# Moved POOL work, a reordered router chain and a new order of two lanes in a two-layer perceiver kernel

## The chip, the core and the metric

The kernel runs on one core of one Trainium2 chip, in one launch. Five engines take part: TensorE (PE), VectorE (DVE), ScalarE (ACT), GpSimd (POOL) and SyncE (SP). Each has its own instruction queue, works through it in order, and waits on semaphores that the others raise. The metric is the device time of one execution in microseconds.

## The reference, cut to what matters

Four sequences of 128 latents with 128 channels (`x`) pass through two layers; a context of 2048 tokens per sequence is attended to in each. Each step adds its result to `x`, after a normalisation of its input.

```python
# layer 0: sampled cross attention (A), retention (B), expert layer (C)
gate_scores = softmax(x @ Wg.T)                    # 8 experts
topk_val, topk_idx = top_k(gate_scores, 2)
comb = one_hot(topk_idx) weighted by topk_val / (topk_val.sum() + EPS)
for e in range(8):
    a, b = split(x @ W1[e].T + b1[e]); g = a * sigmoid(b)
    out = out + (g @ Wo.T + bo) * comb[..., e:e + 1]
# layer 1: masked cross attention (D), a gated retention block (E), expert layer (F)
scores = where(mask == 0, -1e9, q @ k.T / sqrt(8)); out = softmax(scores) @ v
# E: convolution over the batch, silu, q k v g, 2-way router per head, rotary,
#    causal retention, a norm per head, gate, projection, then a silu feed-forward block
# F: router over 8 experts (top 2), gelu(x @ w1[e]) @ w2[e] weighted and summed
```

## The kernel before

**Stages.** `STAGES` A to E follow each other; E holds the second retention and the last expert layer too. The 512 tokens stand as four blocks `b` of 128. Everything is float32 apart from some helpers in bf16. PSUM is one tensor `BK` of 8 banks. The order on each engine is written out by hand as a list of calls, and each call waits on counted semaphores.

**Stage B** is the first retention. PE computes scores (L2058), DVE multiplies them by the decay (L1370), PE multiplies by the values (L2067). `b_s_ps` counts the scores. POOL is nearly idle here.

**Stage C**, the first expert layer. After the norm PE computes the router's logits (L2099). DVE turns them into weights in some twenty small instructions (L1402 to L1432), ACT does one Exp (L797), and `r_cw` counts two marks of DVE: the sum of the weights, and the weights split into three bf16 parts in `CW3`. PE transposes these (L2125), ACT copies them (`CWS`, L801, `c_split`), and `widen_share(e)` (L2117) spreads the weights of expert e over the partitions. Meanwhile `up(e)` (L2109) makes the four hidden tiles of an expert, two pairs (a, b); ACT takes the sigmoid of the b tile (L807), `gated(e, j)` on DVE multiplies (L1397, counted by `e_g`), and `share(e, j)` multiplies by the spread weights (L1440, counted by `c_part`). POOL adds the results of experts 1 to 5 into `SUM` (L631, `c_sum`). PE projects `SUM`, expert 6 and expert 7 with `joined` (L2136) into four banks. Its `proj_ps` marks let DVE add the residual, two blocks at a time (L1024, `both_added`), and begin the next norm.

POOL has other work in stage C: `keys_and_values` builds the block-diagonal keys `QB` (L603), the values `VMD` and `ONEH` for stage D, and L623 and L625 prepare the bias and residual in `XH` that the last add uses.

**Stage D**, the masked cross attention over the last 128 keys, in 16 steps n of four heads. ACT takes the exponentials (L821), PE transposes (`turn(n)`, L2196), ACT or DVE copies the result back (`turned(n)`, L830 or L1737), and `values(b)` (L2212) multiplies by the values (c = 0) and by ones (c = 1, the softmax sums). `divide(b)` (L1475) divides. `project_keys(h)` (L2223, L2227) projects and `looked_up(h)` (L1731) adds.

**Stage E** runs in two lanes h of two blocks each, interleaved with stage D and with each other. Lane h goes through `first_stats`, norm LN_E (L1536), transposes (`lane_norm_T`, L2271), `convolve`, `gate_xT`/`gated_xT`, `project_qkvg` (L2278), `choices`, `shares`, `rotate` on POOL, `weights`, `outputs`, `centred`, `square`, `variances`, `deviation` (a Sqrt), `contexts`, `turn_context`, `project_context`, `attended`, norm LN_E2, `ff_up` (L2302), `gate_ff` (a Tanh) and `gated_ff`, `ff_down` (L2311), `finished`, norm LN_F, `logits`, `chances`, `route` (an Exp), `best_two`. Then come its eight experts: `up(h, e)` (L2329), `gelu(h, e)` (L906), `down(h, e)` (L2344), `weigh(h, e)` (L1724). `down(h, e)` waits for `weigh(h, e - 2)`, since two experts share a bank. Lane 1 is one retention behind lane 0: its retention runs beside the experts of lane 0.

**Warming.** `stay_warm(bk, n)` (L1829) issues n matmuls of the identity whose result nobody reads. `WARM` is 13. ACT holds one set of function tables at a time; a function outside it gets an ACT_TABLE_LOAD ahead of it.

## Time and profile before

| | us |
|---|---|
| runs of the kernel | 279.26, 281.15, 281.96 (median 281.15) |
| the profiled execution | 281.34 |
| its span, first to last instruction | 279.6 |
| busy in the span: PE, DVE, ACT, POOL | 235.5, 191.2, 128.1, 43.2 |
| mean granted TensorE clock | 0.933 |

The profile records one execution. An engine's busy time is the time of its instructions; register, branch, semaphore and DMA-issuing instructions are not counted. A float32 matmul stands as two instructions in the trace. The granted clock is 1.0 at 2.4 GHz and 0.5 at 1.2 GHz.

### The profile page before, as it was taken

Reading aid. Unit: us, or ns where it says so; the run is one execution under the profiler, and the core shown is the slowest. Engines: PE = TensorE matmul, PEld = TensorE weight load, DVE = VectorE, ACT = ScalarE, POOL = GpSimd, SP = SyncE. Lnnn points to the kernel's source line nnn. Section 1 sums busy time; section 2 is a strip of 40 time slices with the busy share of each in tenths; the row PEclk is TensorE's granted clock in tenths of the full one; section 3 lists DMA queues with packets and bytes.
Section 4 is the critical chain, followed back from the end, with each engine's and each line's share of the span. In section 5 each row is a group of like instructions: output and inputs, shape, how many; then the busy total and the mean of one; then the engine's idle time right before and its main releaser. Section 6 shows DMA issues by size and latency. Waiting matters only on the chain.

```text
span 279.6 us, 4964 instructions
## 1 busy us (share of the span) xinstructions
PE 235.5 (84%) x1885; PEld 171.5 (61%) x1885; DVE 191.2 (68%) x550; ACT 128.1 (46%) x274; POOL 43.2 (15%) x65
## 2 busy tenths in 40 slices
PE   8858676957869679699995998759878999999995
PEld 8445453635434565244592564437666999999995
DVE  6998899587578667979866768785779655424111
ACT  1377785644161106233305955762424564363331
POOL 6000000000100038367320001210350010100000
PEclk9999998695597999999999999986995999999999
DMA  6970000003980300000000000000000000000000
GB/s 179 356 295 1 2 4 0 2 2 83 438 382 1 147 6 0 2 0 0 0 4 1 2 2 1 1 2 0 4 0 0 0 4 0 2 0 19 2 0 19
DMA packets 5564, 13.74 MB, mean 49 GB/s; under 512 B 2081, under 2 KB 3745, under 8 KB 4898
## 3 DMA queue, kind: packets, MB, share of 16 engines
q1 hardware_dynamic: 4096, 10.73, 10.3%
q10 hardware_dynamic: 1442, 2.66, 2.9%
q8 instruction: 16, 0.26, 0.4%
q14 instruction: 10, 0.08, 0.1%
HBM read 13.13 MB, written 0.26 MB: 48 GB/s over the span
## 4 chain that ended last, share of the span: by engine, by line
PE 60%; DVE 23%; ACT 9%; issue 4%; POOL 1%; DMA 1%; DVEq 0%; ACTq 0%
PE BK L2329 11%; PE BK L2344 10%; PE BK L2109 7%; PE BK L2212 3%; PE BK L2185 3%; ACT WTF L750 3%; PE BK L2196 2%; DVE WTF L1370 2%; PE BK L1932 2%; PE BK L2136 2%; DVE WTF L1215 2%; PE BK L1829 2%; PE BK L2058 2%; ACT WTF L821 1%; PE BK L2041 1%
## 5 line engine op out<-in xcount | busy, mean ns | idle before, releaser
L2329 PE MATMUL BK<-XT,WTF 128*128 128x256 f32 x128 | 32.8, 404 | 0.0
L2344 PEld LDWEIGHTS BK<-WTF 128*128 128x128 f32 x256 | 30.9, 192 | 0.8
L906 ACT ACTIVATE WTF<-BK 128x512 f32<-128x512 f32 x32 | 18.9, 598 | 26.4 <-PE BK L2329 26.4
L2344 PE MATMUL BK<-WTF 128*128 128x128 f32 x256 | 31.0, 275 | 0.0
L2109 PE MATMUL BK<-XT,WTF 128*128 128x512 f32 x64 | 28.7, 594 | 0.0
L2329 PEld LDWEIGHTS BK<-XT,WTF 128*128 128x128 f32 x128 | 25.0, 205 | 3.2
L1724 DVE SCALAR_TENSOR_TENSOR X<-BK,CW,X 128x128 f32<-128x128 f32 x32 | 9.7, 346 | 24.7 <-PE BK L2344 24.7
L750 ACT ACTIVATE WTF<-BK 128x512 f32<-128x512 f32 x40 | 22.6, 601 | 7.1 <-PE BK L1915 7.0
L597 POOL TENSOR_TENSOR RSTD<-VE,MHALF 128x2 f32<-128x2 f32 x8 | 5.6, 710 | 103.9 <-DVE VE L1043 103.1
L821 ACT ACTIVATE WTF<-BK,MN 128x128 f32<-128x128 f32 x64 | 18.0, 394 | 6.7 <-DVE MN L1469 6.7
L2109 PEld LDWEIGHTS BK<-XT,WTF 128*128 128x128 f32 x64 | 12.0, 190 | 14.1 <-issue 12.8
L1215 DVE TENSOR_SCALAR WTF<-WTF 128x512 f32<-128x512 f32 x40 | 16.5, 421 | 4.9 <-ACT WTF L750 4.5
L807 ACT ACTIVATE KVW<-BK,cols_sb 128x512 f32<-128x512 f32 x16 | 11.0, 688 | 17.7 <-PE BK L2109 17.7
L1932 PE MATMUL BK<-WTF,KVW 128*32 128x160 f32 x256 | 12.9, 326 | 5.8 <-DVE WTF L1215 5.6
L1915 PE MATMUL BK<-R,SELR 128*128 128x128 bf16 x160 | 14.1, 230 | 4.1 <-DVE R L1120 4.1
L1915 PEld LDWEIGHTS BK<-R,SELR 128*128 128x128 bf16 x160 | 10.4, 103 | 9.1 <-issue 5.9
L2196 PE MATMUL BK<-ident,WTF 128*128 128x128 f32 x64 | 10.4, 292 | 5.3 <-ACT WTF L830 2.6
L638 POOL TENSOR_TENSOR RSTD<-VE,MHALF 128x2 f32<-128x2 f32 x6 | 4.2, 700 | 69.0 <-DVE VE L1530 43.6
L2196 PEld LDWEIGHTS BK<-ident,WTF 128*128 128x128 f32 x64 | 7.1, 145 | 11.6 <-ACT WTF L821 8.8
L1397 DVE SCALAR_TENSOR_TENSOR WTF<-BK,cols_sb,KVW 128x512 f32<-128x512 f32 x16 | 11.9, 747 | 3.1 <-ACT KVW L807 3.1
L631 POOL TENSOR_TENSOR WTF<-WTF 128x512 f32<-128x512 f32 x10 | 12.5, 1274 | 8.7 <-DVE WTF L1440 8.7
L1465 DVE TENSOR_REDUCE MX<-BK 128x4 f32<-128x512 f32 x16 | 11.0, 686 | 4.1 <-PE BK L2185 4.1
(309 smaller groups left out, 457.7 us busy)
## 6 DMA issues: line engine op xcount, KB each, us to landing
WTF<-w_f_dram SPq DMA_DIRECT2D x2, 2048.0 KB, 14.5
WTF<-w_c_dram SPq DMA_DIRECT2D x1, 2048.0 KB, 7.7
decay<-c_decay_dram ACTq DMA_DIRECT2D x1, 1024.0 KB, 7.3
decay<-mask_q_dram SPq DMA_DIRECT2D x1, 1024.0 KB, 4.8
crows_sb<-c_rows_dram ACTq DMA_DIRECT2D x1, 544.0 KB, 8.1
w_e_sb<-w_e_dram SPq DMA_DIRECT2D x1, 480.0 KB, 4.8
w_b_sb<-w_b_dram SPq DMA_DIRECT2D x1, 384.0 KB, 5.5
WTF<-win_dram SPq DMA_DIRECT2D x1, 320.0 KB, 6.2
```

The source lines that it names most:

```text
L631: pool.tensor_tensor(SUM[:, j, :], SUM[:, j, :], GT[:, e % 2, 2 + j, :], ALU.add).then_inc(c_sum, 1)
L750: act.activation(WT[:, v % 2, :, :, k, :], sbank(u).rearrange("p (h u q) -> p h u q", h=4, u=4), ACT.Abs)\
L821: ins = act.activation(SS[:, b % 2, h, :], score_bank(n)[:, j * P:(j + 1) * P], ACT.Exp, scale=float(1.0 / np.sqrt(HD)), bias=MN[:, b, h:h ...
L906: act.activation(GT[:, e % 2, 2 * p:2 * p + 2, lane_cols(h)], lane_bank(h, 2 + p).rearrange("p (a n) -> p a n", a=2), ACT.Gelu).then_inc(e ...
L1215: dve.tensor_scalar(w, w, 1.0, -1.0, ALU.min, ALU.add).then_inc(a_w, 1)
L1397: dve.scalar_tensor_tensor(out=GT[:, e % 2, j, :], in0=hbank(2 * p), scalar=ba, in1=SG[:, e % 2, j, :], op0=ALU.add, op1=ALU.mult).then_in ...
L1915: ins = pe.matmul(sbank(u)[:, h * P:(h + 1) * P], SEL[:, NK * h + k, :], R[:, g, a * P:(a + 1) * P], start=True, stop=True)
L1932: ins = pe.matmul(BK[32 * h:32 * h + 32, sample_bank(n), j * NK * QL:(j + 1) * NK * QL], KVW[:, 2 * b + j, 4 * g + h, :, :].rearrange("p f ...
L2109: ins = pe.matmul(hbank(u), w_c1[:, o:o + P], XT[:, :], start=True, stop=True)
L2196: ins = pe.transpose(turn_bank(n)[:, h * P:(h + 1) * P], SS[:, b % 2, 4 * g + h, :], ident[:, :])
L2329: ins = pe.matmul(lane_bank(h, 2 + p)[:, 256 * i:256 * i + 256], w_f1[:, o:o + P], XT[:, lane_cols(h)], start=True, stop=True)
L2344: ins = pe.matmul(lane_bank(h, e % 2)[:, i * P:(i + 1) * P], GT[:, e % 2, j, b * P:(b + 1) * P], w, start=(j == 0), stop=(j == 3))
```

## The change

On POOL the keys and values for stage D are built in stage B, as soon as the buffers are free; the values come first, so the counts of `d_blk` change. L623 and L625 move behind the adds of the experts. The power of LN_F of lane 0 is done in the middle of `rotate(1)`. In stage C half of `up(2)` stands ahead of the wait for `c_split`, the last `widen_share` stands between the halves of `up(7)`, DVE does `share(7, 0)` before `gated(7, 1)`, and the last `joined` is split by `j`. In stage D and E two tiny activations load the tables of Sqrt and Gelu early, `values(3)` is split by `c` around the projection of context 0, the order of the lanes on ACT, DVE and PE changes, and `route(1)` moves behind `gelu(1, 1)`. Warming matmuls: 13 become 11 ahead of stage C, 10 ahead of stage D and 10 ahead of LN_F; the 8 after `project_keys(1)` go.

```diff
-            def keys_and_values():
-                pool.wait_ge(b_o_ps, 4)
+            def last_values():
+                pool.wait_ge(a_ctx, 4)
+                settle(pool.memset(VMD, 0.0))
+                settle(pool.memset(ONEH[:, :, :], 0.0))
+                pool.memset(own(ONEH[:, :, :]), 1.0).then_inc(d_blk, 1)
+                pool.wait_ge(vd_ready, 1)
+                pool.tensor_copy(own(VMD), vd[:, :, :].rearrange("p b (g j d) -> p (b g) j d", g=4, j=4))\
+                    .then_inc(d_blk, 1)
+
+            def last_keys():
+                pool.wait_ge(b_s_ps, 16)
                 pool.wait_ge(kd_ready, 1)
...
                 if s == "B":
                     power(LN_B)
                     pool.memset(CW3[:, :, :, :], 0.0).then_inc(consts_ready, 1)
+                    last_values()
+                    last_keys()
                 if s == "C":
                     power(LN_C)
-                    pool.wait_ge(ln_xhat, xhat_count(LN_C))
-                    keys_and_values()
...
+                    pool.wait_ge(r_cw, 1)
+                    pool.wait_ge(ln_xT_ps, xT_count(LN_C))
+                    pool.wait_ge(loads["crows"], 48)
+                    settle(pool.tensor_tensor(XH[:, :, :], row("ff_bo").unsqueeze(1).to_broadcast([P, B, D]),
+                                              S1[:, :].unsqueeze(2).to_broadcast([P, B, D]), ALU.mult))
+                    pool.tensor_tensor(XH[:, :, :], XH[:, :, :], X[:, :, :], ALU.add).then_inc(xb_ready, 1)
...
                         settle(pool.tensor_tensor(qr, qk, cs[:, 0, pair], ALU.mult))
+                        if meanwhile:
+                            lane_power(*meanwhile)
...
-                    rotate(1)
-                    lane_power(LN_F, 0)
+                    rotate(1, (LN_F, 0))
...
                     exponentials(15)
+                    act.activation(VM[:, :], col("eps"), ACT.Sqrt)
                     turned(14)
                     turned(15)
                     square(0)
                     deviation(0)
+                    act.activation(VM[:, :], col("eps"), ACT.Gelu)
                     context(0)
                     second_xT(0)
+                    gate_ff(0, (0,))
                     gate_xT(1)
-                    gate_ff(0)
+                    gate_ff(0, (1, 2))
                     take_qkvg(1)
+                    last_xT(0)
+                    gelu(0, 0)
                     between(1)
-                    last_xT(0)
+                    gelu(0, 1)
                     route(0)
-                    gelu(0, 0)
-                    gelu(0, 1)
                     square(1)
                     gelu(0, 2)
                     deviation(1)
                     gelu(0, 3)
+                    gelu(0, 4)
                     context(1)
...
                     for e in range(NE):
                         gelu(1, e)
+                        if e == 1:
+                            route(1)
...
+                        if e == NE - 1:
+                            share(e, 0)
+                        if e >= 2:
                             gated(e, 1)
-                        share(e, 0)
+                        if e < NE - 1:
+                            share(e, 0)
...
                     contexts(0)
+                    attended(0)
                     divide(3)
-                    attended(0)
+                    lane_norm(LN_E2, 0, CT)
                     looked_up(1)
                     first_stats(1)
-                    lane_norm(LN_E2, 0, CT)
                     lane_norm(LN_E, 1, X)
                     convolve(1)
+                    gated_ff(0, (0,))
                     gated_xT(1)
-                    gated_ff(0)
+                    gated_ff(0, (1, 2))
                     gated_q(1)
                     finished(0)
+                    lane_norm(LN_F, 0, X)
                     choices(1)
+                    chances(0)
                     shares(1)
-                    lane_norm(LN_F, 0, X)
                     gate_out(1)
                     weights(1)
-                    chances(0)
                     outputs(1)
+                    centred(1)
                     best_two(0)
-                    centred(1)
                     bypass(1)
                     variances(1)
                     weigh(0, 0)
+                    weigh(0, 1)
                     contexts(1)
...
+                    up(2, (0, 1))
                     pe.wait_ge(c_split, 1)
                     widen_share(0)
-                    for e in range(1, NE):
+                    widen_share(1)
+                    up(2, (2, 3))
+                    for e in range(2, NE - 1):
                         widen_share(e)
-                        if e + 1 < NE:
-                            up(e + 1)
+                        up(e + 1, (0, 1) if e == NE - 2 else range(4))
+                    widen_share(NE - 1)
+                    up(NE - 1, (2, 3))
...
+                    pe.wait_ge(c_part, 2 * NE - 1)
+                    for b in range(B):
+                        joined(last, b, False, False, (0,))
                     pe.wait_ge(c_part, 2 * NE)
                     for b in range(B):
-                        ins = joined(last, b, False, True)
+                        ins = joined(last, b, False, True, (1,))
...
-                    values(3)
+                    values(3, (0,))
                     turn_context(0)
                     project_context(0)
+                    values(3, (1,))
                     project_keys(1)
-                    stay_warm(3, 8)
                     lane_norm_T(LN_E2, 0, 1)
                     lane_norm_T(LN_E, 1, 1)
                     ff_up(0)
                     project_qkvg(1)
                     ff_down(0)
-                    stay_warm(3)
+                    stay_warm(3, 10)
                     lane_norm_T(LN_F, 0, 0)
```

Beside the experts of lane 0, each step of lane 1 (`turn_context(1)`, `project_context(1)`, its norms, `ff_up(1)`, `ff_down(1)`) stands one expert later on PE, and `down(0, 7)` comes ahead of `logits(1)` and `up(1, 0)`; ACT and DVE follow the same order.

## Rows read from the trace of the kernel before

**Rows 1.** Page, part 2: granted clock in 40 slices of the span.

```profile
PEclk9999998695597999999999999986995999999999
```

**Rows 2.** Chain that ended last, in order of time: start, us, what.

```profile
138.80 5.36 PE BK L2136 x48
...
212.18 6.08 PE BK L2329 x16
...
220.04 1.73 PE BK L2329 x8
```

**Rows 3.** Timeline of the router chain: start, us, engine, line, operation, count, idle before.

```profile
101.90 1.37 POOL L597 TENSOR_TENSOR RSTD<-VE,MHALF 128x2 f32<-128x2 f32 x2 [29.37 <-DVE VE L1043]
...
103.98 4.03 POOL L603 TENSOR_TENSOR SCR<-kTd,head_sb 128x512 f32<-128x512 f32 x4 [0.72 <-DVE XH L999]
...
107.29 0.77 DVE L1407 TENSOR_TENSOR PR<-EX,S 128x32 f32<-128x32 f32 x1
...
112.01 0.18 DVE L1423 CAST SELR<-RK 128x32 bf16<-128x32 f32 x1
...
112.36 1.04 POOL L623 TENSOR_TENSOR XH<-rows_sb,S 128x512 f32<-128x512 f32 x1 [1.61 <-DVE S L1424]
112.45 0.98 DVE L1427 CAST SELR<-EX 128x32 bf16<-128x32 f32 x1
...
113.48 1.26 POOL L625 TENSOR_TENSOR XH<-XH,X 128x512 f32<-128x512 f32 x1
114.02 0.78 DVE L1431 CAST R<-SELR 128x64 f32<-128x64 bf16 x1
...
114.95 0.64 PE L2125 MATMUL BK<-ident,R 128*96 128x128 f32 x4 [1.89 <-DVE R L1432]
...
116.28 0.60 PE L2117 MATMUL BK<-SELR,gate 96*128 96x512 bf16 x2 [0.69 <-ACT SELR L801]
```

**Rows 4.** Timeline at the end of stage C.

```profile
140.01 1.28 DVE L1440 TENSOR_TENSOR WTF<-BK,WTF 128x512 f32<-128x512 f32 x2
143.38 0.43 DVE L1024 TENSOR_TENSOR X<-BK,XH 128x256 f32<-128x256 f32 x1 [2.09 <-PE BK L2136]
```

**Rows 5.** Timeline from the last turn of stage D to `ff_down(0)`.

```profile
187.90 0.60 ACT L830 ACTIVATE WTF<-BK 128x512 f32<-128x512 f32 x1 [1.27 <-PE BK L2196]
...
188.81 1.28 ACT L874 ACT_TABLE_LOAD   x1
...
190.11 0.32 ACT L874 ACTIVATE SM<-SM,cols_sb 128x32 f32<-128x32 f32 x1
190.26 1.93 PE L2212 MATMUL BK<-WTF,ONEH 128*32 128x128 f32 x32
...
192.25 0.96 DVE L1475 RECIPROCAL KEEP<-BK 128x128 f32<-128x128 f32 x1 [0.91 <-PE BK L2212]
...
195.74 0.42 DVE L1731 TENSOR_TENSOR X<-BK,X 128x256 f32<-128x256 f32 x1 [0.28 <-PE BK L2227]
...
203.46 1.60 PE L2311 MATMUL BK<-w_e_sb,decay 128*128 128x128 f32 x12 [0.30 <-DVE decay L1679]
```

**Rows 6.** Timeline from `shares(1)` to `down(0, 2)`.

```profile
208.88 0.19 DVE L1594 SCALAR_TENSOR_TENSOR SM<-SCR 128x32 f32<-128x32 f32 x1
...
209.48 0.60 DVE L1536 TENSOR_SCALAR XH<-X,MV,RSTD 128x128 f32<-128x128 f32 x2
...
210.14 0.55 PE L2271 MATMUL BK<-ident,XH 128*128 128x128 f32 x2 [2.17 <-DVE XH L1536]
...
220.65 0.61 DVE L1724 SCALAR_TENSOR_TENSOR X<-BK,CW,X 128x128 f32<-128x128 f32 x2
...
225.34 1.95 PE L2344 MATMUL BK<-WTF 128*128 128x128 f32 x16
```

**Rows 7.** Windows: us, then busy of PE, PEld, DVE, ACT, POOL; clock, DMA, GB/s.

```profile
151.50:153.64 2.14, 0.00 (x1) 0.00 (x1) 2.06 (x5) 1.34 (x6) 0.00 (x0) 1.00 0.00 0
...
210.35:217.20 6.85, 6.38 (x18) 5.06 (x17) 6.17 (x19) 3.08 (x5) 0.00 (x0) 0.50 0.00 0
```

More of the change, by code:

```diff
@@ L616, in _ @@
                     pool.memset(CW3[:, :, :, :], 0.0).then_inc(consts_ready, 1)
+                    last_values()
+                    last_keys()
                 if s == "C":
                     power(LN_C)
-                    pool.wait_ge(ln_xhat, xhat_count(LN_C))
-                    keys_and_values()
-                    pool.wait_ge(r_cw, 1)
-                    pool.wait_ge(loads["crows"], 48)
-                    settle(pool.tensor_tensor(XH[:, :, :], row("ff_bo").unsqueeze(1).to_broadcast([P, B, D]),
-                                              S1[:, :].unsqueeze(2).to_broadcast([P, B, D]), ALU.mult))
-                    pool.tensor_tensor(XH[:, :, :], XH[:, :, :], X[:, :, :], ALU.add).then_inc(xb_ready, 1)
                     for e in range(1, NE - 2):
@@ L644, in _, with rotate @@
                     flat = lambda a: a.rearrange("p b a n -> p b (a n)")
-                    def rotate(h):
+                    def rotate(h, meanwhile=None):
                         pair = lane_pair(h)
@@ L950, in _ @@
                     gelu(0, 3)
+                    gelu(0, 4)
                     context(1)
-                    gelu(0, 4)
+                    gelu(0, 5)
                     second_xT(1)
-                    gelu(0, 5)
+                    gelu(0, 6)
                     gate_ff(1)
-                    gelu(0, 6)
+                    gelu(0, 7)
                     last_xT(1)
-                    gelu(0, 7)
-                    route(1)
                     for e in range(NE):
                         gelu(1, e)
+                        if e == 1:
+                            route(1)
         @block.vector
@@ L2126, in _, with joined @@
                     ins.then_inc(c_wide_ps, 1)
+                    up(2, (0, 1))
                     pe.wait_ge(c_split, 1)
                     widen_share(0)
-                    for e in range(1, NE):
+                    widen_share(1)
+                    up(2, (2, 3))
+                    for e in range(2, NE - 1):
                         widen_share(e)
-                        if e + 1 < NE:
-                            up(e + 1)
-                    def joined(src, b, start, stop):
-                        for j in range(2):
+                        up(e + 1, (0, 1) if e == NE - 2 else range(4))
+                    widen_share(NE - 1)
+                    up(NE - 1, (2, 3))
+                    def joined(src, b, start, stop, js=(0, 1)):
+                        for j in js:
                             ins = pe.matmul(BK[:, (2, 3, 4, 6)[b], 0:P], src(j)[:, b * P:(b + 1) * P],
@@ L2197, in turn, with values @@
                         ins.then_inc(d_pT_ps, 1)
-                    def values(b):
+                    def values(b, cs=(0, 1)):
                         pe.wait_ge(d_pT, (2, 4, 8, 12)[b])
@@ L2203, in values @@
                         if b == 0:
-                            pe.wait_ge(d_blk, B + 2)
+                            pe.wait_ge(d_blk, 2)
                         if b == 3:
                             pe.wait_ge(d_om, 3)
-                        for c in range(2):
+                        for c in cs:
                             for j in range(4):
```

42 lines of the change are left out of this document (18 added, 24 removed).

## The prediction

> **What bounds the kernel now.** I read the clock row of the page first: TensorE is granted full speed nearly everywhere, with dips around slices 10, 13, 27 and 31 [rows 1]. Then the chain that ended last, in order of time. It runs on PE through the first expert layer, where the eight experts end in one unbroken piece of 48 matmul instructions, 5.36 us, and again from 212.18 to the end of the span, where each further expert step of 8 instructions takes 1.73 us [rows 2]. The first 16 instructions of that last stretch took 6.08 us; at 1.73 us for 8 they would take 3.46. So there are two kinds of place where time can be won: the stretches in which PE waits before such a piece begins, and the low-clock stretches. The timeline then shows who is late in each place, and windows show the clock [rows 3 to 7].
>
> **Part 1, the router chain.** Between the logits and the weights that `widen_share` spreads, DVE works through a string of tiny instructions. A cast of 32 columns takes 0.18 us; three of the tiny ones took 0.77, 0.98 and 0.78 us instead, and each ended within 0.1 us of the end of a POOL `tensor_tensor`: L1407 at 108.06 beside L603 (to 108.01), L1427 at 113.43 beside L623 (to 113.40), L1431 at 114.80 beside L625 (to 114.74) [rows 3]. That is (0.77-0.18) + (0.98-0.18) + (0.78-0.18) = 2.0 us of waiting for POOL. The change takes all three POOL jobs away: L603 and its neighbours go to stage B, L623 and L625 go behind the adds of the experts. So `r_cw` comes at 112.9, not 114.9.
>
> The second gain is PE's hole. The four transposes end at 115.59 and the first `widen_share` starts at 116.28, after ACT's copy [rows 3]: 0.69 us. `up(2, (0, 1))` now stands in it; what it needs (`e_g` 2) is `gated(0, 1)`, which DVE does before `r_cw`. I count 0.6 of it. Sum of part 1: -2.6 us for PE at the start of the experts. Does it last? PE is busy without a break from there to 144.16, and DVE finishes the last share at 141.29 (L1440, 140.01 + 1.28), 1.0 us before PE reaches the matmuls that need it, at about 142.3 [rows 2, 4]. DVE's shares start only about 0.9 us earlier than now, since `widen_share(0)` comes behind half of `up(2)`, so DVE loses 1.7 us of its distance in the first experts. The 1.0 us at the end is the way of the last pair itself (PE, sigmoid, `gated`, `share`), not a backlog of DVE, so I expect it to stay; if the 1.7 were carried to the end, PE would wait 0.7 and -1.9 would be left. I keep -2.6; the bounds are -0.6 (POOL was not the cause) and -2.7.
>
> **What the moved POOL work costs in stage B.** POOL is idle for 29.37 us before the power of LN_C at 101.90 [rows 3]. `last_values` (memset 1.8 us, a copy) falls where DVE has nothing pressing. `last_keys` waits for the last scores, about 91.2, and its 4.03 us end at 95.3, ahead of the power that is queued behind it. Beside it DVE runs operations that read PSUM; L1440, of the same kind, takes its 0.64 us in the expert stage, where POOL adds all the time [rows 4]. Cost 0; if one were held, at most one POOL instruction, 1.0 us. The keys' other waiters are in stage D, long after. If `last_keys` came 7 us late it would hold the power of LN_C.
>
> **Part 2, the last pair.** `share(7, 0)` before `gated(7, 1)` and the split of `joined(last, ...)` shorten the way from the last share to the projection. But PE gets there last, 1.0 us after DVE (above), so nothing waits that could be shortened: 0. The split has a price instead. Now the two matmuls of block 0 and of block 1 precede those of 2 and 3, so the first half is free four matmuls before the end; DVE starts its add at 143.38, 0.8 us before PE ends [rows 4]. With `js` outermost it is free only two before the end. 48 instructions in 5.36 us [rows 2] are 0.22 us for each of the 24 matmuls, so this is +0.45 us for the add, and all that follows to the norm of stage D hangs on it. The 10 warming matmuls in place of 13 then just make sure that PE is not late itself: 0. Bounds for part 2: 0 to +0.45; I take +0.45, since nothing but DVE's and POOL's own short steps stands between that add and the norm.
>
> **Part 3, the end of the second retention.** Times are those of the profile of before. (a) A dummy Sqrt now stands ahead of `turned(14)`. The table load is 1.28 us and the tiny activation about 0.2 us, so `turned(14)`, `turn(15)`, `turned(15)` (187.90) and `values(3)` come 1.5 us later [rows 5]. In exchange `deviation(0)` finds its table there: the load at 188.81 goes. Context 0 is ready at about 192.1, and `project_context(0)` keeps its place. (b) The second half of `values(3)`, 1.93 us at the low clock and about half at the full one, now follows it, so `divide(3)` starts at 195.5 to 196.0 where it started at 192.25, and `looked_up(1)` moves from 195.74 to 197.6 to 198.1: +1.9 to +2.4 us [rows 5]. On PE `ff_up(0)` is queued behind the transposes of that lane's norm, so `ff_up(0)` and `ff_down(0)` (203.46) move by the same amount; I take +1.9. (c) The norm of LN_F of lane 0 now follows its statistics at once, on DVE and on POOL (in the middle of `rotate(1)`, whose rest waits meanwhile, with `weights(1)` behind it, which is not due until later). PE's wait of 2.17 us ahead of the transposes at 210.14 nearly goes: -2.1 [rows 6]. (d) Then the experts may start at 211.4 instead of 212.18, at full clock: -0.8 and -2.6. But DVE is late next. `between(1)` stands behind `gelu(0, 0)`, so `shares(1)` can start at about 211.4 + 1.73 + 1.0 = 214.1. From its first instruction at 208.88 to the end of the first `weigh` (220.65 + 0.61) DVE took 12.4 us, of which some 1.2 are the norm, the chances and pauses [rows 6]. So `weigh(0, 0)` ends at 214.1 + 11.2 = 225.3, and `down(0, 2)`, which needs it, started at 225.34 before [rows 6]. The 3.4 us are waited away there. From there both orders are PE work without a break, and the later order of lane 1 and of `route(1)` (two table loads beside PE's 3.5 us per expert) adds no wait. Part 3: 0, with bounds -0.8 and +0.5 while the clock behaves.
>
> What a table load costs decides (a). The trace has the load at 188.81 and the next activation at 190.11, 1.30 us later [rows 5]. The Trainium skill ("ScalarE: Activation LUTs", What ACT_TABLE_LOAD costs) adds a drain of about 1.38 us to every switch, 2.66 us in all; by that, `values(3)` would come 2.9 us later and the sum would be 1.4 us worse. The row shows no such drain.
>
> **Sum.** The profiled execution took 281.34 us, span 279.6 and 1.74 around it, which stays. 281.34 - 2.6 + 0.45 + 0 = 279.2 us. It lies 0.2 above the median of the three runs, 281.15; I keep 279.2.
>
> **The rivals.**
> *Clock, slower side.* The change drops 8 warming matmuls between `project_keys(1)` and the next transposes, and leaves PE idle there for about 2.4 us (198.2 to 200.6 by the moves above); after the start of the second experts it leaves another pause of 2.6 us while `gelu(0, 2)` and `weigh(0, 0)` are late. PE's pause of 2.17 us before 210.14 was followed by the low level, 1.2 GHz, in the window from 210.35 to 217.20; a pause of 2.14 us at 151.50 was not [rows 7]. So it can go either way. One such stretch over work that bounds costs 6.08 - 3.46 = 2.6 us [rows 2]: 279.2 + 2.6 = 281.8. It decides when PE rests over some 2 us in one of the two places with the clock falling behind it; both together give 284.4. The Trainium skill ("TensorE: Matmul & The Clock Gate", Part 1) says that half rate is the default and that activity releases it; by that rule alone removed warming matmuls can only hurt, with the same 281.8.
> *Lane order wins.* If the Sqrt and the second half of `values(3)` hide better than I think, so that `looked_up(1)` is not later, the 2.1 us of (c) are kept: 279.2 - 2.1 = 277.1. For it: in (b) the low clock makes up nearly 1 us. Against it: three engines' queues all put lane 1 behind `values(3)`.
> *It doesn't do what it says.* The three long DVE instructions are long for another reason than POOL. Then part 1 is -0.6 and the time is 281.34 - 0.6 + 0.45 = 281.2. Against it: three coincidences within 0.1 us.
>
> **Chances.** Forecast 0.42 (278.4 to 280.2 by its bounds), clock 0.27, lane order 0.23, not POOL 0.08. The range reaches into the rivals on both sides, to 277.0 and to 282.8. About 1% (2.8 us) is what a measurement of this kernel can tell from no change. Faster by more means below 278.3: nearly all of the lane-order case and a little of the forecast, 0.27. Slower means above 284.0: both clock stretches, 0.10. Within: 0.63.
>
> **What would show it.** In the profile of the changed kernel: L1407, L1427 and L1431 at about 0.2 us, and no gap between the transposes and `up(2)`; the experts of the first layer starting 2.6 us earlier and still that much ahead at their end; the first add of stage D less than 0.5 us before PE's end; a table load ahead of `turned(14)`; `looked_up(1)` late and PE idle before the transposes of lane 1; no 2.17 us pause before LN_F; a wait of PE for ACT and DVE before `up(0, 3)` and `down(0, 2)`. The prediction is wrong if the clock falls in one of those pauses, or if DVE's distance in the first experts is used up, so that PE waits for `gated` there.

## The result and the profile after

The changed kernel takes 289.38 us, the median of four executions (287.37 to 290.95). The kernel before, timed beside it, took 281.55 us. The ratio is 1.0306 with a 95% interval of 1.024 to 1.0373: slower by 3%. Here and in the table of the experiments a median is that of all executions, while a ratio leaves out those over 1.5% above the fastest of their kernel. The profiled execution of the changed kernel took 287.37 us, with a span of 285.6 us.

The clock row of its page answers to [rows 1].

```profile
PEclk9999997997799799999996899955599989999999
```

Slices 27 to 29, 7.1 us each, stand at half speed, where before had an 8, a 6 and a 9; slice 22 has a 6, where before had a 9. The low slices of before at 8, 10, 11 and 31 are higher here. The slices count from 1. The granted clock averaged over the four executions is 0.911. I cut both traces at the same events to see where the 6.0 us between the two profiles arose. The times in this table are starts of instructions, the last one the end of the last operation ahead of the output DMA; the last column is the run e5, explained with the experiments.

| stretch, from one event to the next | before | after | difference | values late |
|---|---|---|---|---|
| start to the norm of stage B | 71.28 | 69.55 | -1.7 | 69.53 |
| to the norm of stage C | 31.34 | 33.42 | +2.1 | 30.13 |
| to the norm of stage D | 43.48 | 41.06 | -2.4 | 41.07 |
| to the second part of `values(2)` | 35.21 | 38.35 | +3.1 | 38.39 |
| to `up(0, 0)` | 30.72 | 33.60 | +2.9 | 30.12 |
| to `down(0, 2)` | 13.31 | 15.18 | +1.9 | 12.17 |
| to the end | 52.02 | 52.23 | +0.2 | 52.02 |

**Router chain.** The timeline of the changed kernel answers to [rows 3], this time with the router instructions alone:

```profile
107.63 0.19 DVE L1416 TENSOR_TENSOR PR<-EX,S 128x32 f32<-128x32 f32 x1
112.20 0.18 DVE L1436 CAST SELR<-EX 128x32 bf16<-128x32 f32 x1
112.96 0.18 DVE L1440 CAST R<-SELR 128x64 f32<-128x64 bf16 x1
113.30 0.64 PE L2139 MATMUL BK<-ident,R 128*96 128x128 f32 x4
141.31 0.42 DVE L1033 TENSOR_TENSOR X<-BK,XH 128x256 f32<-128x256 f32 x1 [2.73 <-PE BK L2154]
```

All three long instructions are short, and stage C is 2.4 us shorter. The last row is the first add of stage D: PE ended at 141.65, so it starts 0.34 us before PE's end where in the kernel before it started 0.78 us ahead [rows 4].

**Stage B.** The timeline around its norm:

```profile
70.47 2.22 DVE L1008 TENSOR_SCALAR XH<-X,MV,RSTD 128x128 f32<-128x128 f32 x2 [0.33 <-POOL RSTD L597]
70.74 1.81 POOL L601 MEMSET KEEP<- 128x2048 f32 x1
72.69 0.44 PE L1836 MATMUL BK<-ident,XH 128*128 128x128 f32 x2 [2.15 <-DVE XH L1008]
73.87 5.40 PE L2055 MATMUL BK<-XT,w_b_sb 128*128 128x512 f32 x8 [0.75 <-ACT XT L702]
```

The second pair of the norm takes 2.22 us, and it ends 0.14 us after the end of the moved memset of `VMD` on POOL. PE waits 2.15 us for it. Behind that pause the clock is low, as the windows below show. In the kernel before, the same memset stood in stage C, beside instructions of the router chain, and held none of those that began behind it. L1409 took 0.43 us beside it, and the same instruction takes 0.43 us in the changed kernel with no memset beside it:

```profile
107.95 1.80 POOL L605 MEMSET KEEP<- 128x2048 f32 x1
108.10 0.43 DVE L1409 TENSOR_TENSOR SELR<-PR 128x256 f32<-128x256 f32 x1
```

**End of the retention.** The chain that ended last, in order of time, from the dummy Sqrt (L938) to `ff_down(0)` (L2333):

```profile
187.23 1.28 ACT L938
188.72 0.49 ACT WTF L835
189.35 1.10 PE BK L2217 x4
...
194.32 1.22 PE BK L2314 x4
195.54 1.87 PE BK L2233 x32
197.41 1.15 PE BK L1847 x2
198.55 1.15 PE BK L2245 x4
199.71 0.87 PE BK L2249 x4
201.05 0.50 DVE STAT L1534 x2
...
203.56 0.69 PE BK L2293 x2
204.25 4.11 PE BK L2324 x12
```

Windows of it: us, then busy of PE, PEld, DVE, ACT, POOL; clock, DMA, GB/s.

```profile
74.00:77.40 3.40, 3.40 (x5) 1.32 (x6) 0.69 (x1) 0.00 (x0) 0.09 (x1) 0.51 1.00 429
152.80:159.20 6.40, 6.40 (x20) 3.16 (x19) 3.00 (x6) 3.84 (x15) 0.00 (x0) 0.50 0.00 0
186.80:207.20 20.40, 14.27 (x98) 10.32 (x97) 10.98 (x36) 6.72 (x14) 2.73 (x4) 0.50 0.00 1
227.70:231.10 3.40, 3.40 (x8) 2.77 (x9) 3.16 (x12) 3.28 (x4) 0.00 (x0) 0.50 0.00 0
```

For 20.4 us without a break TensorE has 1.2 GHz. In this stretch the links that run on PE cost 1.5 to 1.8 times what they do at 2.4 GHz: the projections 1.22 us instead of 0.71, a half of `values` 1.94 instead of 1.06. `looked_up(1)` comes at 200.60 (before: 195.74 [rows 5]), `ff_down(0)` at 209.73 (203.46). What `divide(3)` waits for is the second half of `values(3)`, as its row in the timeline says:

```profile
195.47 1.94 PE L2233 MATMUL BK<-WTF,ONEH 128*32 128x128 f32 x32
195.58 0.42 DVE L1680 TENSOR_TENSOR CT<-BK,WTF 128x256 f32<-128x256 f32 x1 [2.48 <-PE BK L2314]
197.47 0.96 DVE L1488 RECIPROCAL KEEP<-BK 128x128 f32<-128x128 f32 x1 [0.47 <-PE BK L2233]
```

**Experts of lane 0.** Timeline of the changed kernel, against [rows 6]:

```profile
214.60 0.44 PE L2293 MATMUL BK<-ident,XH 128*128 128x128 f32 x2 [1.03 <-DVE XH L1549]
...
225.28 0.42 ACT L875 ACTIVATE WTF<-WTF 128x256 f32<-128x256 f32 x1 [3.35 <-DVE WTF L1651]
225.71 1.28 ACT L911 ACT_TABLE_LOAD   x1
...
227.66 2.93 PE L2351 MATMUL BK<-XT,WTF 128*128 128x256 f32 x6 [2.59 <-ACT WTF L911]
```

`up(0, 3)` waits 2.59 us for `gelu(0, 2)`, which stands on ACT behind `square(1)`; that one waits 3.35 us for DVE's chain of lane 1.

### The profile page after: what moved, and what is told of

It is laid out like the page before. It is cut to its first block, busy times and chain, and to the rows that moved or that the text cites. A ratio compares the mean times of both kernels' runs of the same rounds, so it can differ in the third digit from the quotient of the medians.

```text
span 285.6 us, 4904 instructions
## 1 busy us (share of the span) xinstructions
PE 235.7 (83%) x1853; PEld 168.9 (59%) x1853; DVE 190.9 (67%) x550; ACT 129.4 (45%) x277; POOL 43.3 (15%) x65
## 4 chain that ended last, share of the span: by engine, by line
PE 58%; DVE 23%; ACT 11%; issue 3%; POOL 2%; DMA 1%; DVEq 0%; ACTq 0%; POOLq 0%
PE BK L2123 10%; PE BK L2351 9%; PE BK L2366 9%; PE BK L2206 3%; DVE WTF L1379 3%; ACT WTF L755 3%; PE BK L2233 3%; PE BK L2217 3%; PE BK L2324 2%; PE BK L2154 2%; POOL RSTD L597 2%; PE BK L1946 2%; DVE WTF L1224 2%; ACT WTF L826 1%; PE BK L2197 1%
## 5 line engine op out<-in xcount | busy, mean ns | idle before, releaser
L2351 PE MATMUL BK<-XT,WTF 128*128 128x256 f32 x128 | 32.1, 398 | 2.6 <-ACT WTF L911 2.6
L2351 PEld LDWEIGHTS BK<-XT,WTF 128*128 128x128 f32 x128 | 24.0, 199 | 6.3 <-ACT WTF L911 3.2
L2123 PEld LDWEIGHTS BK<-XT,WTF 128*128 128x128 f32 x64 | 12.0, 190 | 13.3 <-issue 12.2
L1224 DVE TENSOR_SCALAR WTF<-WTF 128x512 f32<-128x512 f32 x40 | 16.5, 420 | 4.6 <-ACT WTF L755 4.2
L2217 PE MATMUL BK<-ident,WTF 128*128 128x128 f32 x64 | 11.8, 321 | 6.7 <-ACT WTF L835 4.0
L1929 PE MATMUL BK<-R,SELR 128*128 128x128 bf16 x160 | 13.4, 222 | 4.1 <-DVE R L1129 4.1
L2217 PEld LDWEIGHTS BK<-ident,WTF 128*128 128x128 f32 x64 | 8.1, 160 | 13.8 <-ACT WTF L826 7.0
L1929 PEld LDWEIGHTS BK<-R,SELR 128*128 128x128 bf16 x160 | 9.7, 98 | 9.0 <-issue 5.8
L702 ACT ACTIVATE XT<-BK 128x512 f32<-128x512 f32 x4 | 2.4, 597 | 24.2 <-PE BK L1836 21.9
## 6 DMA issues: line engine op xcount, KB each, us to landing
WTF<-w_f_dram SPq DMA_DIRECT2D x2, 2048.0 KB, 14.4
```

Source lines behind the costliest of these rows:

```text
L1224: dve.tensor_scalar(w, w, 1.0, -1.0, ALU.min, ALU.add).then_inc(a_w, 1)
L1929: ins = pe.matmul(sbank(u)[:, h * P:(h + 1) * P], SEL[:, NK * h + k, :], R[:, g, a * P:(a + 1) * P], start=True, stop=True)
L2123: ins = pe.matmul(hbank(u), w_c1[:, o:o + P], XT[:, :], start=True, stop=True)
L2217: ins = pe.transpose(turn_bank(n)[:, h * P:(h + 1) * P], SS[:, b % 2, 4 * g + h, :], ident[:, :])
L2351: ins = pe.matmul(lane_bank(h, 2 + p)[:, 256 * i:256 * i + 256], w_f1[:, o:o + P], XT[:, lane_cols(h)], start=True, stop=True)
```

## The experiments

The result of each is the median, and the ratio to the kernel before on the same chip with its 95% interval. "Clock" is the granted clock averaged over the executions; that of before was 0.937 to 0.941 in these runs, two executions of 352 and 568 us left out.

| run | median us | ratio | interval | clock |
|---|---|---|---|---|
| e1 router | 284.78 | 1.0195 | 1.0066 to 1.0323 | 0.921 |
| e2 lanes | 286.98 | 1.0224 | 1.0102 to 1.0347 | 0.918 |
| e3 warm | 286.23 | 1.0216 | 1.0069 to 1.0363 | 0.931 |
| e4 no dummy | 288.72 | 1.0262 | 1.0103 to 1.0422 | 0.914 |
| e5 values late | 279.62 | 0.9965 | 0.9927 to 1.0002 | 0.943 |
| e6 late, warm | 279.87 | 0.9956 | 0.9910 to 1.0002 | 0.940 |
| e7 whole join | 280.10 | 0.9980 | 0.9935 to 1.0025 | 0.933 |
| e8 POOL only | 284.27 | 1.0135 | 1.0067 to 1.0204 | 0.929 |
| e9 retention half | 284.95 | 1.0124 | 1.0044 to 1.0204 | 0.916 |
| e10 expert half | 280.17 | 0.9957 | 0.9910 to 1.0003 | 0.940 |
| e11 norm early | 281.92 | 1.0014 | 0.9972 to 1.0056 | 0.938 |
| e12 no eight | 282.14 | 1.0038 | 0.9989 to 1.0087 | 0.927 |
| e13 no dummies in e9 | 284.41 | 1.0134 | 1.0090 to 1.0179 | 0.920 |
| e14 whole values in e9 | 284.00 | 1.0095 | 1.0057 to 1.0133 | 0.928 |
| e16 expert half mended | 279.42 | 0.9941 | 0.9909 to 0.9972 | 0.941 |
| e17 order only | 283.48 | 1.0107 | 1.0063 to 1.0151 | 0.926 |
| e18 changed, values late | 285.22 | 1.0155 | 1.0086 to 1.0223 | 0.919 |

### The two halves, the warming and the dummies

The theory at this point: the memset on POOL takes back most of the router's gain, and the order at the end of the retention is late by itself. The rivals: the missing warming matmuls are the whole cause, or one half of the change is.

e1 has parts 1 and 2 (POOL's moves in stages B and C, the router order, the last pair, warming of 11 and 10), with the lanes of before.

> Parts 1 and 2 alone: the POOL moves, the router chain, the last pair, 11 and 10 warming matmuls; stage D and E in the order of before. Theory A (hold and order): the memset in stage B takes back 1.6 us, the chain gives 2.5 us, the split of the join takes 0.45, and the low stretch at the start of stage D (3.1 us) is a result of the shorter warming and the new timing there: 281.5 + 1.6 - 2.5 + 0.45 = 281.1 us without that stretch, 284 with it. Rival 1 (the lane order is all of it): 279.5. Rival 2 (warming is the cause everywhere): 284.

e2 has part 3 only, with stages A to C of before.

> Part 3 alone: the order of the lanes, the two dummy activations, values(3) split, the 8 warming matmuls gone; stages A to C as before. Theory A: values(3) comes 1.6 us later, looked_up(1) 4.9 us later, and both lanes start the last experts late: 281.5 + 6 = 287.5 us. Rival 1 (all of it is here): 289.5. Rival 3 (nothing of it is here, it's clock luck in stages B to D): 281.5.

e3 is the changed kernel with all its warming back.

```diff
-stay_warm(3, 11)
+stay_warm(3)
-stay_warm(1, 10)
+stay_warm(1)
 project_keys(1)
+stay_warm(3, 8)
-stay_warm(3, 10)
+stay_warm(3)
```

> The changed kernel with the warming matmuls of before: 13, 13, 8 after project_keys(1), 13. Rival 2 (the clock falls because PE rests where warming was taken away): 282 us, with the full clock from 190 us on. Theory A: the order is late by itself; the 8 matmuls shorten the low stretch after 187 us a little and cost nothing: 287 to 289 us.

e4 is the changed kernel without the two dummy activations.

```diff
-act.activation(VM[:, :], col("eps"), ACT.Sqrt)
-act.activation(VM[:, :], col("eps"), ACT.Gelu)
```

> The changed kernel without the two dummy activations, so turned(14) is not held by the table load. If the load ahead of turned(14) is the first cause of the delay (values(3) +1.6 us and the pause that lets the clock fall): 285 to 287 us, the full clock back before 200 us. If the split of values(3) and the order behind it are the cause: 289 us as the changed kernel, since deviation(0) then loads its table itself.

e1 and e2 are both slower than before, by 2.0% and 2.2%, so neither rival of a single half holds. The full warming gives back 0.9 points of the 3.06 (2.5 us), and e3 stays clearly slower than before, so missing warming isn't the whole cause; whether it is any part, e3 can't tell, since its interval reaches from 1.0069 to 1.0363. Without the dummies 0.4 points are gone, which the intervals can't tell from zero either.

### The memset in stage B

e5 is e1 with one semaphore changed: POOL's memset now waits until the rotary products of stage B are done.

```diff
 def last_values():
-    pool.wait_ge(a_ctx, 4)
+    pool.wait_ge(b_rot, 2)
     settle(pool.memset(VMD, 0.0))
```

> Parts 1 and 2, with the memset of the values on POOL held until the rotary products of stage B are done, so that it runs beside DVE operations that read PSUM. Nothing else differs from the router kernel. Theory (the memset holds the second pair of the norm of stage B for 1.6 us, and PE's pause behind it lowers the clock): the pair of TENSOR_SCALAR takes 0.6 us again, the stage starts 1.6 us earlier, 1.6 to 2.5 us less than the router kernel, which was 284.8 us: 282.3 to 283.2. Rival (the hold is absorbed later in stage B, where DMA or the scores set the pace): 284.5.

e5 takes 279.62 us, e1 284.78, a gain larger than either theory had. The timeline of e5, against the one of the changed kernel:

```profile
70.45 0.60 DVE L1003 TENSOR_SCALAR XH<-X,MV,RSTD 128x128 f32<-128x128 f32 x2 [0.33 <-POOL RSTD L597]
70.92 0.52 PE L1830 MATMUL BK<-ident,XH 128*128 128x128 f32 x2 [0.41 <-DVE XH L1003]
...
72.18 3.70 PE L2049 MATMUL BK<-XT,w_b_sb 128*128 128x512 f32 x8 [0.74 <-ACT XT L701]
...
77.73 1.80 POOL L601 MEMSET KEEP<- 128x2048 f32 x1 [6.95 <-DVE KEEP L1361]
78.96 1.29 DVE L1374 TENSOR_TENSOR WTF<-BK,decay 128x512 f32<-128x512 f32 x2 [1.28 <-PE BK L2066]
```

The pair takes 0.60 us again, and the projections behind it 3.70 us where the changed kernel needed 5.40, at the higher clock: the window from 74.0 to 77.4 stands at 1.00 here and at 0.51 there. Both profiles reach this norm at the same time, 69.53 and 69.55, so this is a clean comparison: the last column of the table has stage B 3.3 us shorter. The memset now runs mostly in a pause of DVE; the first of two products that read PSUM overlaps its last 0.6 us, and the two keep their 0.65 us each.

Between e1 and e5 the medians differ by 5.2 us and the ratios by 2.3 points, where e1's interval alone is 1.3 points wide to either side. Of this 1.6 us are the hold, and the average clock of the executions rose from 0.921 to 0.943. The profiles bear out more than the hold. From the norm of stage B to that of stage D all five with the memset at this norm (changed kernel, e1, e3, e4, e8) take 74.2 to 74.5 us; the twelve that have both the later memset and the router order take 70.3 to 72.5, 71.3 on average. So it costs about 3 us there, half of it the hold. That the pause is what lowers the clock is likely, not shown: all five have a low stretch that begins 1.2 to 1.6 us after PE's pause, but e2 and e14 have one at the same place (76.3 and 76.4) without the hold, and in both profiles of before and in e6 and e12 the clock is low there already.

e8 is before with POOL's moves alone, the early memset included.

> Before, with the POOL moves alone (values and keys in stage B, the two bias and residual jobs behind the adds); PE, DVE and ACT in the order of before, all warming as before. Theory: the three router instructions take 0.2 us each, weights 2.0 us earlier, but the memset holds the norm of stage B for 1.6 us: sum -0.4, 281.0 us. Rival (POOL was not the cause of the long router instructions): they stay at 0.8 us, 283 us.

It is 1.35% slower, 284.27 us where 281.0 was expected, with the router 2 us shorter (from the norm to the transposes 10.33 us, before 12.33) and the norm's pair again at 2.22 us. From the norm of stage B to that of stage D its profile has 74.45 us, before 74.82: hold and gain nearly cancel, as expected. What makes it slower than before stands ahead of the norm of B (1.2 us) and behind that of D (1.3 us), outside the steps that it moves.

e18 makes the same one-line repair in the changed kernel.

> The changed kernel (289.4 us) with one edit, the memset of the values waits for the rotary products of stage B. If the costs add up as in the router kernel (5.2 us there): 284.2 us. If there is only the hold itself of 1.6 us and the rest of the difference was chance: 287.8 us.

285.22 us instead of 289.38: 4.2 us, near the value that adds up.

### Warming and the join in stage C

e6 is e5 with 13 warming matmuls in place of 11 and 10.

> As the values-late kernel, with 13 warming matmuls ahead of stage C and of stage D instead of 11 and 10. Theory (the shorter warming lets the clock fall more often, at 153 and 98 us): mean clock over the executions back from 0.92 to 0.94, 280.0 us. Rival (the falls are chance): the same as the values-late kernel, 282.5 us.

279.87 against 279.62 us: no effect of that warming can be measured there. The theory that its lack made the clock fall is not borne out. e7 is e6 with the last join whole.

```diff
-pe.wait_ge(c_part, 2 * NE - 1)
-for b in range(B):
-    joined(last, b, False, False, (0,))
 pe.wait_ge(c_part, 2 * NE)
 for b in range(B):
-    ins = joined(last, b, False, True, (1,))
+    ins = joined(last, b, False, True)
```

> As the one before (late values, 13 and 13), with the join of the last pair whole again, all four matmuls of a block together. Forecast of the split's price: the first add of stage D starts 0.8 us before PE's end instead of 0.34, and the time is 0.45 us less: 279.5 us. Rival (the split lets PE start half of the join before the last share is done, and saves that wait): equal, or 0.3 us more.

280.10 against 279.87 us. The 0.45 us that the trace shows for the split is too small for this comparison, in either direction.

### Part 3 in halves, on a sound base

The base for what follows is e6, 279.87 us. e9 adds the end of the retention, with the 8 warming matmuls kept.

> Base is the kernel with late values and 13 and 13 warming matmuls (279.9 us), all 8 warming matmuls after project_keys(1) kept. Added: only the first half of part 3, the order at the end of the retention (two dummy activations, values(3) split around the projection of context 0, attended(0) and the norm LN_E2 ahead of divide(3) and looked_up(1), gate_ff split). Theory (this order is late by itself: from values(2) to the start of the last experts the changed kernel with full warming took 31.0 us where before took 30.7, though its early norm LN_F should save 2.1): +2.4, 282.3 us. Rival (only the missing warming made it late): 279.9 us.

e10 adds the early norm of LN_F and the new order of the experts.

> Same base (279.9 us). Added: only the second half of part 3, the norm LN_F of lane 0 right behind its statistics, between(1) behind gelu(0, 0), and lane 1 one expert later on PE, ACT and DVE. Theory (the early norm saves 2.1 us, but the first gelus stand ahead of between(1), shares(1) to centred(1) start late and with them square(1), gelu(0, 2) and weigh(0, 0): from the start of the experts to down(0, 2) 15.1 us where the base takes 12.2): -2.1 + 2.9 = +0.8, 280.7 us. Rival (PE is busy there anyway): 277.8 us.

e12 takes only the 8 warming matmuls out of the base.

> Same base (279.9 us), only the 8 warming matmuls after project_keys(1) taken away. Theory (the 3.1 us between the changed kernel and the one with full warming come from these 8): the clock stays low from about 190 to 205 us, mean clock 0.93 instead of 0.943, 282.5 us. Rival (the clock falls there because of the late order, the 8 don't matter): 279.9 us.

The first half costs 1.7 points (4.7 us), twice the expected 2.4 us. The second costs nothing. Taking the 8 matmuls out costs 0.8 points (2.3 us), near the 2.6 expected; the two intervals just overlap. In e12 PE pauses 2.10 us ahead of the transposes, where the base pauses 0.31 us, and the windows that follow stand at different levels, first e12's, then the base's:

```profile
200.00:203.60 3.60, 3.60 (x11) 2.68 (x10) 2.22 (x6) 1.82 (x4) 0.00 (x0) 0.54 0.02 5
```

```profile
200.00:203.60 3.60, 3.60 (x17) 2.59 (x15) 2.96 (x8) 2.44 (x5) 0.22 (x1) 1.00 0.01 2
```

`ff_up(0)` takes 4.44 us in e12 and 2.75 us in the base.

### Which piece of the retention half

e13 is e9 without the dummies, e14 is e9 with `values(3)` whole ahead of `turn_context(0)`, e17 is e9 with both undone. Only this is left in e17:

```diff
 contexts(0)
-divide(3)
 attended(0)
+divide(3)
+lane_norm(LN_E2, 0, CT)
 looked_up(1)
 first_stats(1)
-lane_norm(LN_E2, 0, CT)
 lane_norm(LN_E, 1, X)
```

with `gate_ff(0)` and `gated_ff(0)` split around the same step of lane 1.

> The retention half (285.0 us, ratio 1.0124) without its two dummy activations. Theory S (the table load ahead of turned(14) makes PE pause and lowers the clock over all that follows): turn(15) and values(3) 1.5 us earlier, full clock before 195 us, 281.5 us. Theory V (the second half of values(3) in front of project_keys(1) is what costs): the delay of lane 1 stays and deviation(0) loads its table itself, 284 to 285 us.

> The retention half (285.0 us) with values(3) whole ahead of turn_context(0), dummies kept. Theory V: divide(3) 2 us earlier and with it looked_up(1), 282 us. Theory S: the clock falls anyway, and context 0 now waits for all of values(3): 285 us or more.

> The retention half (285.0 us) without the dummies and with values(3) whole: what is left is attended(0) and the norm LN_E2 ahead of divide(3) and looked_up(1) on DVE, and gate_ff(0) split on ACT. Theory (the dummy Sqrt and the split of values(3) hold the loss between them, each brings its own late turn or late lane 1 and the low clock makes both dearer): the base again, 279.9 us. Rival (the order on DVE costs: divide(3) now waits for the projection of context 0, and project_keys(1) behind it comes 1 to 2 us later): 282 us.

Neither repair brought much. e13 came out where theory V had it, but e14, which takes V's cause away, came out at 284.00 us where V had 282. e17 says why. The order alone makes 1.0107, where the whole half has 1.0124. Its timeline:

```profile
194.14 0.42 DVE L1676 TENSOR_TENSOR CT<-BK,WTF 128x256 f32<-128x256 f32 x1 [2.58 <-PE BK L2310]
...
195.48 0.95 DVE L1484 RECIPROCAL KEEP<-BK 128x128 f32<-128x128 f32 x1
196.47 0.35 DVE L1485 SCALAR_TENSOR_TENSOR CTT<-BK,NOTF,KEEP 128x128 f32<-128x128 f32 x1
...
198.13 0.42 DVE L1740 TENSOR_TENSOR X<-BK,X 128x256 f32<-128x256 f32 x1 [0.81 <-PE BK L2245]
```

```profile
196.87 1.23 PE L2245 MATMUL BK<-w_d_sb,CTT 128*128 128x128 f32 x4 [1.50 <-DVE CTT L1485]
```

`attended(0)` (L1676) waits 2.58 us for PE's projection of context 0, and DVE idles, with `divide(3)` (L1484, L1485) queued behind it although its input has been there since 192.4. In the base `divide(3)` starts at 193.36, as soon as its input is there, and is over before `attended(0)` at 194.88. So PE waits 1.50 us for `divide(3)`, and the clock is low from within that wait on (0.64 on average from 197.5 to 205.0). `looked_up(1)` then waits for PE, so the norm that was put ahead of it isn't what holds it. From `values(2)` to `up(0, 0)` e17 takes 33.8 us, the base 30.1.

With the split, though, this order decides nothing. In e9, as in the changed kernel, `attended(0)` is over before the second half of `values(3)` is, and `divide(3)` starts as soon as that ends:

```profile
192.72 1.94 PE L2231 MATMUL BK<-WTF,ONEH 128*32 128x128 f32 x32
192.82 0.42 DVE L1678 TENSOR_TENSOR CT<-BK,WTF 128x256 f32<-128x256 f32 x1 [2.48 <-PE BK L2312]
194.72 0.96 DVE L1486 RECIPROCAL KEEP<-BK 128x128 f32<-128x128 f32 x1 [0.46 <-PE BK L2231]
```

So there are two edits that each make `divide(3)` late: the split on PE, and, where the split is undone, the order on DVE. In the profiles `looked_up(1)` comes 14.4 us after `values(2)` in the base, 16.6 in e17 (order alone), 16.5 in e13 (order and split) and 18.2 in e9, with the dummies too, where PE pauses 2.40 us ahead of the last turn. The ratios of e9, e13, e14 and e17 can't be told apart by their intervals. What the split or the dummies would cost with the order of before wasn't tried.

### The expert half

e11 takes only the early norm of LN_F of lane 0, on the base, with `chances(0)` and `between(1)` left where they were relative to the rest.

> Same base (279.9 us). Added: only the norm LN_F of lane 0 right behind its statistics (on POOL in the middle of rotate(1), on DVE ahead of choices(1), on ACT last_xT(0) ahead of between(1)), everything else in the order of before. Theory (PE's wait of 2.2 us ahead of LN_F goes, shares(1) is 0.6 us later): 277.8 us, no low stretch behind it. Rival (the chain through shares, outputs, centred, square, weigh(0, 0) is what ends last, so that the wait only moves to down(0, 1) or down(0, 2)): 279.9 us.

e16 is e10 with three moves.

```diff
 route(0)
+gelu(0, 2)
 square(1)
-gelu(0, 2)
-deviation(1)
 gelu(0, 3)
+deviation(1)
...
 best_two(0)
+weigh(0, 0)
 bypass(1)
 variances(1)
-weigh(0, 0)
```

> The expert half (280.2 us) with three moves: gelu(0, 2) ahead of square(1) and gelu(0, 3) ahead of deviation(1) on ACT, weigh(0, 0) ahead of bypass(1) and variances(1) on DVE. Theory (PE waits 2.6 us for gelu(0, 2), which is queued behind the chain of lane 1, then 0.4 for weigh(0, 0)): up(0, 3) starts at once, down(0, 2) 1.3 us earlier, 278.9 us. Rival (best_two(0), behind centred(1), holds weigh(0, 0) all the same and the later variances(1) delay lane 1): 280.2 us.

`up(0, 0)` starts 28.3 and 28.4 us after `values(2)` in e10 and e11, 30.1 in the base: the early norm brings 1.8 us. From `up(0, 0)` to `down(0, 2)` then come 14.1 us in e10, 16.4 in e11, 12.2 in the base, so both give it back, and e11, with 281.92 us, lies above both of its forecasts. In e11 `gelu(0, 0)` is behind `route(0)`, which waits for DVE, and PE waits at the second step already:

```profile
215.49 2.67 PE L2345 MATMUL BK<-XT,WTF 128*128 128x256 f32 x8 [3.72 <-ACT WTF L911]
```

e16 has this in its timeline instead of e10's wait of 2.58 us:

```profile
216.47 1.89 PE L2346 MATMUL BK<-XT,WTF 128*128 128x256 f32 x8
220.32 3.03 PE L2361 MATMUL BK<-WTF 128*128 128x128 f32 x16 [1.95 <-DVE X L1734]
```

The wait for `gelu(0, 2)` is gone; `down(0, 2)` comes 12.8 us after `up(0, 0)` (e10 14.1), as expected, and now waits 1.95 us for `weigh(0, 0)`. The gain is lost again in its profile: the clock is low behind that wait (0.60 from 220.3 to 224.6), and from `down(0, 2)` to the end it takes 54.1 us, e10 52.3. The time is 279.42 us, 0.9941 with an interval that ends at 0.9972. It is the one version whose interval lies wholly below 1, if by 0.6% only, and it can't be told from e6 (0.9956) or e10 (0.9957).

### Before, a second profile

> The kernel before, a second profile of it. If the low stretch at the start of stage D is chance: it may stand in this profile too, with the scores there at 2.08 us instead of 1.13 and some 3 us lost there, and other stretches elsewhere full; time anywhere from 278.3 to 283.7. If it comes from the change: no low stretch at 153 to 160 us.

It took 281.25 us. Its clock row is the same as that of [rows 1], and it has no low stretch at the start of stage D either. All 18 profiles of kernels with any part of the change have it, e2 too, whose stages A to C are those of before: there the second pair of scores takes 2.07 to 2.08 us instead of 1.13. This is the +3.1 of the table. It is not the shorter warming ahead of stage D, for e2 and e6 have all 13. Why the two profiles of before escape it isn't settled. Both have low slices earlier, at 8, 10 and 11 (49 to 77 us), and a low stretch later, at 210 to 217 us, that e5 doesn't have: from `values(2)` to `down(0, 2)` e5 takes 42.3 us, before 44.0. So part of the +3.1 comes back, and e5 is not slower than before. The -1.7 of the table's first line is chance: the code ahead of the norm of stage B is the same in all kernels, and their profiles reach it anywhere from 69.5 to 73.0 us. Neither is laid to any edit.

## Why the prediction was wrong

**Part 1, the router chain** was right: the three instructions at 0.18 and 0.19 us, and 2.0 us for them. From the transposes to PE's end of the stage it is 28.35 us, before 29.21: 0.86, where 0.6 was counted for the hole. DVE's distance was not used up.

**What the moved POOL work costs in stage B** is the first step that failed: `last_values` "falls where DVE has nothing pressing", at a cost of 0. It fell on the second pair of the norm that all of stage B waits for: 1.6 us held, a pause of PE, and more time at the low clock behind it. The later memset took 4.2 us off the median of the changed kernel (e18) and 5.2 off that of e1 (e5); the profiles have about 3. The wait on `a_ctx` is met before that norm, so the place could have been read from the list of POOL. The prediction had three cases of DVE instructions that end with POOL's, took the cause to be POOL, and did not ask which DVE instructions the moved ones would meet. `last_keys` did as said: 4.03 us beside reads of PSUM, ahead of the power of stage C.

The Trainium skill ("SBUF — State Buffer", Who interferes with whom) says that copies, casts and `tensor_scalar` can run in a mode that takes the port pair shared with GpSimd, and that the second to issue is blocked for the whole of the first. The rows agree in the main: a `TENSOR_SCALAR` from SBUF to SBUF lasts until a memset of 1.81 us is over, operations that read PSUM are not held. By that rule the hold of 1.6 us was to be expected. They don't bear out that the order of issue decides: by the times of the trace the first of the pair began at 70.47, the memset at 70.74, and both of the pair last until the memset's end.

**Part 2** was right in the trace (+0.45 us for the first add), and too small to be measured.

**Part 3** is the second step that failed. It put (a) to (d) at 0 together; from `values(2)` to `down(0, 2)` the changed kernel is 4.8 us later. (a) was right in size: `turned(15)` is 1.5 us later against `values(2)`, and the table load is 1.28 us with the next activation 0.01 us behind it (187.23, 188.52), so no drain. (b) is the term that failed. It had the right wait, `divide(3)` for the second half of `values(3)`, but the wrong size: against `values(2)`, `divide(3)` is 4.1 us late, where 3.2 to 3.8 were counted, and `looked_up(1)` 3.8 us, where 1.9 to 2.4 were counted and 1.9 taken. It counted 2.1 us from `divide(3)` to `looked_up(1)`, which is what e3 and e18 have, where TensorE is back at 2.4 GHz by then; in the changed kernel, at 1.2 GHz, it is 3.1. So 1.0 of the 3.8 us is the clock behind `divide(3)`, and with the later links `ff_down(0)` is 5.2 us late. (b) also missed that `divide(3)` had been put behind `attended(0)`, whose input comes later; the split hides this in the changed kernel, but e17 shows that without the split it alone costs 1.5 points. The whole half costs 1.7 points (e9). (c) counted 2.1 us for the early norm; e10 shows 1.8. (d) said that these are waited away since DVE and ACT are late next, which is what e10 and e11 show. It gave 13.9 us to `down(0, 2)`; it is 15.2.

**The clock rival** was right that it can only cost: both pauses it named are in the trace, 2.57 us ahead of the transposes of lane 1 and 2.59 us ahead of `up(0, 3)`, and low stretches with them. But it was sized at one stretch of 2.6 us for each, 284.4 us for both, and the measured time lies 5 us above that. The chain at 1.2 GHz for 20.4 us makes every late step later. The 8 removed matmuls are worth 2.3 us by e12; e3 has 2.5 of the 8.6 us (3.06 points) for all the removed warming, within its noise. The Trainium skill ("TensorE: Matmul & The Clock Gate", Part 1) has half rate as the default and activity releasing it; e12 agrees in direction, e5 against e6 shows no effect of the warming at two other places.

The range ended at 282.8 us because part 3 was put at 0 "while the clock behaves", and the clock was a case of its own. In these traces they go together: around the 1.50 us that the order makes PE wait in e17 a low stretch of 6.8 us begins, which the base doesn't have.

Added up, memset 1.5 to 2.3 points, retention half 1.7, warming 0.8, router and join -0.4, make 3.6 to 4.4, and the whole is 3.06. Each of these has an uncertainty of half a point or more, so whether they overlap (a stretch that is low already can't be lowered again) isn't shown.

## What to carry

Before a POOL job is moved, look up which DVE instructions run at the new place, above all in the norm at a stage's start: a `TENSOR_SCALAR` from SBUF to SBUF can be held for as long as the job lasts, and all that waits for it too, while a `TENSOR_TENSOR` beside the same memset was not. In a queue written by hand, a step that only waits must not stand ahead of one whose input is there; compare when the input of each is due, not how long each takes. When two edits each delay the same step, undoing one shows nothing: undo both, then one at a time. Where TensorE is on the chain, count a new pause like those here (2.1 to 2.6 us) as a risk of a low clock over the work behind it, and take a few cheap matmuls out of such a pause only after a run has shown that they do nothing there. A sum made with matmul times at 2.4 GHz is to be made at 1.2 GHz too where the clock has been low just before.

## What the hardware showed

A memset on POOL, which only writes, holds a `TENSOR_SCALAR` of DVE: 2.22 us instead of 0.60 for the pair, in all five profiles that had the two together. Neither a product that reads PSUM (0.65 us) nor a `TENSOR_TENSOR` from SBUF to SBUF (0.43 us) was held beside the same memset. A low stretch can last: 20.4 us at 1.2 GHz with PE busy for 14.27 of them in the changed kernel, 17.0 us with 13.34 in e9. And two profiles of the kernel before, taken apart from each other, had the same clock row slice for slice, although its executions spread from 278 to 285 us, two far ones (352 and 568 us) aside.
